# Centring moved back, last blocks in dead keys, setup signs on VectorE, and a wait in front of the gelu splits

## The reference

```
x = x + attn(layernorm(x))
x = x + ffn(layernorm(x))
attn: Q, K, V = x @ W.T + b      # W is 256 x 256
      scores = Q K^T / 16 * gaussian_mask(key position)
      out = softmax(scores) V, then @ Wo.T + bo
ffn:  h = gelu(x @ (alpha1 * sign(w1)).T + b1)      # 1024 wide
      out = h @ (alpha2 * sign(w2)).T + b2
```

## Time and profile before

| what | value |
|---|---|
| median of 3 runs | 1558.59 us |
| profiled execution | 1560.72 us, span 1558.9 us |
| mean granted TensorE clock | 0.97 |
| PE busy | 1465.9 us, 94% |
| DVE, POOL, ACT busy | 1098.1, 1045.1, 885.6 us (70, 67, 57%) |
| chain of waits | PE 70%, POOL 9%, DVE 7%, ACT 6%, DMA 3% |

### The profile page before, as it was taken

How to read it: one execution, slowest core, us unless ns; L and a number is a source line. 1 busy time by engine, 2 the same in 40 slices (tenths; PEclk the granted TensorE clock), 3 DMA queues, 4 the chain that set the end, 5 groups by cost and what they waited for, 6 DMA issues and landing times.

```text
span 1558.9 us, 21094 instructions
## 1 busy us (share of the span) xinstructions
PE 1465.9 (94%) x7709; PEld 1258.8 (81%) x7709; DVE 1098.1 (70%) x1574; ACT 885.6 (57%) x1238; POOL 1045.1 (67%) x1036
## 2 busy tenths in 40 slices
PE   7789999999898999989999899999999999899997
PEld 5678878788787878878788787878878788788886
DVE  6757766677776768867678776767766678666654
ACT  4566565565655656555565656666555565656433
POOL 4857757676676666766677676765766677576744
PEclk9899999999999999999999999999999999999998
DMA  6633707355062542606445063552716446072431
GB/s 194 97 81 55 154 9 118 99 79 138 22 130 66 95 122 49 152 17 109 109 80 137 10 122 85 89 129 36 144 37 109 108 65 152 1 122 68 70 66 28
DMA packets 107939, 138.50 MB, mean 89 GB/s; under 512 B 11822, under 2 KB 95164, under 8 KB 107836
## 3 DMA queue, kind: packets, MB, share of 16 engines
q1 hardware_dynamic: 107808, 137.15, 42.5%
q10 hardware_dynamic: 28, 0.01, 0.0%
HBM read 37.49 MB, written 16.78 MB: 35 GB/s over the span
## 4 chain that ended last, share of the span: by engine, by line
PE 70%; POOL 9%; DVE 7%; ACT 6%; DMA 3%; SPq 2%; issue 2%; DVEq 0%; POOLq 0%; ACTq 0%
PE ps L1009 19%; PE ps L983 17%; PE ps L1073 9%; PE ps L1086 6%; PE ps L1032 6%; PE ps L1087 5%; POOL kl L381 3%; DMA probs<-g 3%; POOL nmr L407 2%; SPq L306 2%; PE ps L1052 2%; ACT kh L500 2%; PE ps L963 2%; PE ps L964 2%; PE ps L966 2%
## 5 line engine op out<-in xcount | busy, mean ns | idle before, releaser
L389 POOL TENSOR_TENSOR probs<-probs 128x512 fp32r<-128x512 f32 x256 | 343.8, 1366 | 197.3 <-ACT probs L521 197.3
L1009 PE MATMUL ps<-probs,xnh 128*128 128x512 f32 x1024 | 286.0, 394 | 9.7 <-ACT probs L521 9.7
L1086 PE MATMUL ps<-sgn,probs 128*128 128x256 f32 x1024 | 250.9, 286 | 4.6 <-DVE ys L798 2.9
L1087 PE MATMUL ps<-sgn,probs 128*128 128x256 f32 x1024 | 249.1, 284 | 0.0
L754 DVE STREAM_TRANSPOSE probs<-probs 128x1024 f32<-128x1024 f32 x128 | 158.8, 1241 | 109.6 <-DMA probs<-g 108.2
L1009 PEld LDWEIGHTS ps<-probs,xnh 128*128 128x128 f32 x1024 | 190.2, 189 | 51.1 <-issue 13.3
L521 ACT ACTIVATE probs<-probs 128x1024 fp32r<-128x1024 f32 x128 | 135.7, 1060 | 153.1 <-DVE probs L754 152.5
L560 ACT ACTIVATE g<-ps,cols,alpha 128x512 f32<-128x512 f32 x256 | 183.5, 771 | 66.6 <-PE ps L1073 66.5
L515 ACT ACTIVATE g<-ps,nmax 128x1024 f32<-128x1024 f32 x128 | 142.1, 1112 | 123.6 <-DVE nmax L742 122.8
L742 DVE TENSOR_REDUCE nmax<-ps 128x1 f32<-128x1024 f32 x128 | 155.5, 1215 | 78.5 <-PE ps L983 78.2
L1086 PEld LDWEIGHTS ps<-sgn,probs 128*128 128x128 f32 x1024 | 197.0, 192 | 10.0 <-DVE ys L798 4.2
(11 more groups left out here) (115 smaller groups left out, 2770.3 us busy)
## 6 DMA issues: line engine op xcount, KB each, us to landing
probs<-g SPq DMA_DIRECT2D x512, 128.0 KB, 3.5
xrow<-in_L_attn_x_dram SPq DMA_DIRECT2D x32, 512.0 KB, 8.5
xin<-in_L_attn_x_dram SPq DMA_DIRECT2D x32, 512.0 KB, 8.7
out_dram<-xin SPq DMA_DIRECT2D x31, 512.0 KB, 4.5
regrouped_rows<-xn SPq DMA_DIRECT2D x120, 128.0 KB, 5.2
w1s<-in_L_ffn_w_dram SPq DMA_DIRECT2D x1, 1024.0 KB, 7.9
w2s<-in_L_ffn_w_dram SPq DMA_DIRECT2D x1, 1024.0 KB, 10.0
mask_bc<-mask_dram SPq DMA_DIRECT2D x1, 512.0 KB, 6.7
```

Source lines behind the costliest of these rows:

```text
L389: pool.tensor_tensor(ptl(b, q)[:, half(n)], pt(b, q)[:, half(n)], pth(b, q)[:, half(n)].bitcast(F32), ALU.subtract).then_inc(ptl_set, 1)
L1009: last = pe.matmul(ps[:, PV_BANK + c, :], xv[:, j, tile(c)], probs[:, lo, first:first + TH, tile(j)], start=k == 0, stop=k == len(parts) - 1)
L1086: pe.matmul(bank, probs[:, 0, r, tile(j)], sgn2[:, j, :], start=j == 0, stop=False)
L1087: last = pe.matmul(bank, probs[:, 1, r, tile(j)], sgn2[:, j, :], start=False, stop=j == J - 1)
```

## The change

- `center_attention(b+2)` on DVE moves from behind `lo_rows_ffn(b, 0)` to behind `row_max(b+1, 0)`.
- In front of `split_pair(b, 0)` DVE waits for `nmr2_set`, all eight of the batch (the roots of the second norm).
- Query tile 7 is regrouped into `last_regrouped`, which lies over `kl`; the wait for `pv_summed` moves from SP to DVE's `turn_probs(b, 7)`.
- PE does the scores of tiles 6 and 7 back to back, and `weigh_rows` steps 12 to 24 after them.
- Setup: the signs of w2 move from POOL to DVE, in two instructions; the means of |w2| move on ACT from the start to batch(0), in front of those of |w1|; `bvb` and `perm` are made earlier; the product for the bias and `Nh` goes ahead of `scores(0, 0)`; other instructions of the setup change places.

```diff
             def regrouped(b, q):
+                if q == T - 1 and b < B - 1:
+                    return last_regrouped[:, 0, :]
 # SP, regroup_probs
-                if q == T - 1 and b < B - 1:
-                    sp.wait_ge(pv_summed, N2 * b + 1)
-                elif q == T - 1:
+                if q == T - 1 and b == B - 1:
                     sp.wait_ge(kl_set, N2 * (b + 1))
                 if b == 0 and q == 5:
-                    sp.wait_ge(signs2_set, 1)
+                    sp.wait_ge(alphas_set, C)
 # POOL, setup
-            pool.tensor_scalar(sw2[:], w2s[:], 0.0, None, ALU.is_gt).then_inc(pos2_set, 1)
-            pool.wait_ge(alphas_set, C)
-            pool.tensor_scalar(w2s[:], w2s[:], 0.0, None, ALU.is_lt).then_inc(neg2_set, 1)
-            pool.tensor_tensor(sw2[:], sw2[:], w2s[:], ALU.subtract).then_inc(signs2_set, 1)
...
 # ACT, setup
             exponentials(0, 3)
+            normalize_attention(1, range(2, TH))
+            hi_probs(0, 1)
+            exponentials(0, 4)
             signs1(range(0, 2))
...
+            normalize_attention(1, tiles_of(1))
+            def mean_sizes():
+                act.wait_ge(signs_set, 2)
+                for c in range(C):
+                    act.activation(w2s[:, c, :], w2s[:, c, :], ACT.Abs, scale=1.0 / H,
+                                   accum_out=alpha2[:, c:c + 1]).then_inc(alphas_set, 1)
 # DVE, turn_probs
+                if q == T - 1 and b < B - 1:
+                    dve.wait_ge(pv_summed, N2 * b + 1)
 # DVE, setup
             turn_probs(0, 3)
+            dve.tensor_scalar(sw2[:], w2s[:], 0.0, None, ALU.is_lt).then_inc(neg_set, 1)
+            dve.wait_ge(neg_set, 2)
+            dve.scalar_tensor_tensor(out=sw2[:], in0=w2s[:], scalar=0.0, in1=sw2[:], op0=ALU.is_gt,
+                                     op1=ALU.subtract).then_inc(signs_set, 1)
 # DVE, batch
                 lo_rows_ffn(b, 0)
-                if b + 2 < B:
-                    center_attention(b + 2)
                 lo_outputs(b, 1)
                 invert_sums(b, 1)
                 for q in tiles_of(1):
                     add_attention(b, q)
+                dve.wait_ge(nmr2_set, T * (b + 1))
                 split_pair(b, 0)
...
                 row_max(b + 1, 0)
+                if b + 2 < B:
+                    center_attention(b + 2)
                 lo_rows_ffn(b, 1)
 # PE, batch, 0 < b < 15
-                    for i in range(TH):
-                        scores(b, TH + i)
-                        weigh_rows(b, 0, range(6 * i, 6 * i + 6))
+                    scores(b, 4)
+                    weigh_rows(b, 0, range(0, 6))
+                    scores(b, 5)
+                    weigh_rows(b, 0, range(6, 12))
+                    scores(b, 6)
+                    scores(b, 7)
+                    weigh_rows(b, 0, range(12, 24))
```

More of the change, by code:

```diff
@@ L73, in preln_attention_ffn @@
             sb("gap_kmf", [P, S], F32, place)
-            junk2 = sb("junk2", [P, C, H], F32, place)
+            sb("gap_j", [P, C, H], F32, place)
             sb("gap_b", [P, J // 2, D], F32, place)
@@ L85, in preln_attention_ffn @@
         kh = sb("kh", [P, N2, C, HALF], F32R)
+        with ExitStack() as place:
+            last_regrouped = sb("last_regrouped", [P, N2, S], F32, place)
         kl = sb("kl", [P, N2, C, HALF], F32R)
@@ L169, in preln_attention_ffn @@
             sem(n) for n in ("x2_turned", "x2h_set", "x2l_set", "hidden", "gelu_set", "gh_set", "gl_set"))
-        pos2_set, neg2_set, signs2_set = (sem(n) for n in ("pos2_set", "neg2_set", "signs2_set"))
         ffn_summed, ffn_scaled, y_set, table_loaded = (
@@ L596, in _ @@
             act.activation(Nh[:].rearrange("p c d -> p (c d)"), ps[:, 7, :], ACT.Copy).then_inc(nh_set, 1)
[L597 to L600, removed]
             exponentials(0, 1)
@@ L603, in _ @@
             exponentials(0, 2)
-            normalize_attention(1, range(2, TH))
             hi_probs(0, 0)
             exponentials(0, 3)
+            normalize_attention(1, range(2, TH))
+            hi_probs(0, 1)
+            exponentials(0, 4)
             signs1(range(0, 2))
[L608 to L611, removed]
+            exponentials(0, 5)
             hi_probs(0, 2)
+            hi_probs(0, 3)
             signs1(range(2, 2 * C))
[L614 to L618, removed]
+            normalize_attention(1, tiles_of(1))
[4 more added lines that the diff above has]
+                                   accum_out=alpha2[:, c:c + 1]).then_inc(alphas_set, 1)
                 for j in range(J):
@@ L639, in batch @@
                     exponentials(b, 5)
+                if b == 0:
+                    mean_sizes()
                 hi_probs(b, 4)
-                if b == 0:
-                    mean_sizes1()
                 exponentials(b, 6)
@@ L821, in _ @@
                                      op1=ALU.subtract).then_inc(ml_set, 1)
+            dve.wait_ge(consts_set, 5)
+            for c in range(C):
+                dve.tensor_scalar(bvb[:, c, :], ones[:], bv_c[:, c:c + 1], None, ALU.mult).then_inc(bvb_set, 1)
+            dve.tensor_copy(perm[:].rearrange("p (g r) -> p g r", r=QUAD),
+                            ident[:].rearrange("p (r g) -> p g r", r=QUAD)).then_inc(perm_set, 1)
             for n in range(N2):
@@ L834, in _ @@
             dve.tensor_scalar(sw1[:], w1s[:], 0.0, None, ALU.is_lt).then_inc(neg_set, 1)
+            row_max(0, 1)
+            center_attention(1)
             dve.wait_ge(neg_set, 1)
@@ L837, in _ @@
                                      op1=ALU.subtract).then_inc(signs_set, 1)
[L838 to L842, removed]
+            row_max(0, 2)
+            turn_probs(0, 0)
+            row_max(0, 3)
             dve.wait_ge(nh_set, 1)
@@ L845, in _ @@
                               Nh[:].rearrange("p c d -> p (c d)").bitcast(F32), ALU.subtract).then_inc(nl_set, 1)
-            row_max(0, 2)
-            turn_probs(0, 0)
-            row_max(0, 3)
             turn_probs(0, 1)
@@ L853, in _ @@
             dve.tensor_tensor(bias_bc[:], ps[:, 6, 0:D], bias_bc[:], ALU.add).then_inc(bias_set, 1)
+            row_max(0, 5)
             turn_probs(0, 2)
-            row_max(0, 5)
             turn_probs(0, 3)
[L857 to L861, removed]
+            dve.wait_ge(w2_loaded, 16)
+            dve.tensor_scalar(sw2[:], w2s[:], 0.0, None, ALU.is_lt).then_inc(neg_set, 1)
+            dve.wait_ge(neg_set, 2)
+            dve.scalar_tensor_tensor(out=sw2[:], in0=w2s[:], scalar=0.0, in1=sw2[:], op0=ALU.is_gt,
+                                     op1=ALU.subtract).then_inc(signs_set, 1)
             def batch(b, more):
@@ L882, in batch @@
                 if b == 0:
+                    dve.wait_ge(alphas_set, C)
+                    for c in range(C):
+                        dve.tensor_scalar(diag[:, c, :], ident[:], alpha2[:, c:c + 1], None, ALU.mult).then_inc(diag_set, 1)
                     dve.wait_ge(alpha2_spread, 1)
@@ L1121, in _ @@
             last.then_inc(wo_turned, 1)
-            scores(0, 0)
             pe.wait_ge(woT_set, 1)
@@ L1138, in turn_signs1 @@
                     last.then_inc(signs_turned, 1)
-            scores(0, 1)
-            scores(0, 2)
-            turn_signs1(range(0, 2))
             pe.wait_ge(bvb_set, C)
@@ L1146, in _ @@
             last.then_inc(bias_summed, 1)
-            scores(0, 3)
+            for q in range(TH):
+                scores(0, q)
+            turn_signs1(range(0, 2))
             scores(0, 4)
@@ L1161, in turn_signs2 @@
                     if k == 0:
-                        pe.wait_ge(signs2_set, 1)
+                        pe.wait_ge(signs_set, 2)
                     if k < 2:
@@ L1175, in batch @@
                     weigh_rows(b, 0, range(0, 6))
+                    scores(b, 6)
                     turn_signs2(range(0, 2))
-                    scores(b, 6)
                     weigh_rows(b, 0, range(6, 12))
```

5 lines of the change are left out of this document (removed).

## The result

The changed kernel takes **1550.06 us** (median of 5 runs, 1544.87 to 1552.51), the kernel before 1559.85 us on the same chip. The ratio is 0.9934 with an interval of 0.9907 to 0.9961: 0.7% faster. The forecast was 1548. The profiled execution has a span of 1548.3 us and a mean granted clock of 0.975.

The account below looks back on a forecast made before the run. PE bounds the kernel, so time is won only where it idles or runs at its lower clock. -12 + 2.9 + 1.5 - 3 = -10.7 gives 1550.0 profiled, 1548 us as median; range 1508 to 1569, likeliest case 1537 to 1559.

Parts of the forecast that it names:

- stall at `project` gone: PE's wait at project(b, 1) for DVE's lo_outputs, behind the centring: shrinks from 3.3 us to 0.3 in batches 0 to 13.
- next stall without the wait: PE's transposes L1052, late because of POOL's roots: idle 1.26 us, as the old batch 14 shows, unless DVE waits for them.
- new stall, hidden pair 4: PE waits for DVE's L781, late because the first split waits for roots and meets POOL's subtraction: 3.0 us, 15 times.
- clock: PE's lower granted clock after the new stall: 1.7 us a batch, in proportion to the old 1.9; bounds 0 and 3.3.
- a batch, times 14: Batches 0 to 13: 93.2 us each against 94.1, so -0.9 a batch and -12 us in all.
- batch 14: The batch with no centring to move, so nothing to win: 93.2 against 90.3 us, +2.9.
- end: Batch 15, bound by split 3 before ffn_row(0): splits start 1.8 us later, +1.5 us in all, bounds 0 and +3.
- setup: Start up to batch 1's queries: DMAs 5.7 us earlier, less 2.1 for means of |w2| and 0.6 for clock: -3.
- dead keys, score order: Last block regrouped into dead keys, and scores 6 and 7 back to back: both costed at nothing.
- rival A: Old stall goes, L781 late by only 1.0 us, no clock loss: 89.5 a batch, 1492 us; chance 0.17 with half-way cases.
- Rival B: Slower: POOL's third subtraction precedes split 2's TENSOR_TENSOR, stall 4.0, clock 2.2, 94.7 a batch, 1571 us; chance 0.11.

## Why the prediction was right

The mechanism was the one forecast, and the sum came out to 0.1 in the profiled executions (-10.7 and -10.7; the medians of five differ by 9.8). That closeness is luck: its terms were off by -2.2 (start), +1.2 (the fourteen intervals), +1.8 (batch 14) and -0.8 (end), which cancel, and the last two hang on where the clock happened to fall.

| step | predicted | measured | in short |
|---|---|---|---|
| stall at `project` gone | 3.3 to 0.3 | not in the list of waits | right |
| next stall without the wait | 1.26 at the transposes | 1.3 and 1.26 in the two kernels without it | right |
| new stall, hidden pair 4 | 3.0, 15 times | 3.06 in the steady batches, 2.98 in batch 14 | right |
| clock | 1.7 a batch | 1.6 | right |
| a batch, times 14 | 93.2, -12 | 93.33, -10.8 | right |
| batch 14 | +2.9 | +4.7 | undersized |
| end | +1.5 | +0.7; 2.1 like for like in clock | right in kind, a little undersized |
| setup | -3 | -5.2 (-6.5 from the queries of batch 0) | undersized |
| dead keys, score order | 0 | 0 within the error | right |

*The new stall.* The chain through batch 14's times put CAST and TENSOR_TENSOR at 3.97 us behind a wait; they took 3.99 (1418.38 to 1422.37). It put the split 1.8 later, and it waited 1.69. What decided between 1.0 and 3.0 was whether POOL's subtraction holds the split up. The kernel with the subtractions late settles it: same wait, stall 1.21 instead of 3.06. It also comes near rival A's time (1496.6, forecast 1492): the rival was wrong on what POOL does at that instant, not on what it would be worth. Rival B needed POOL's third subtraction ahead of split 2's TENSOR_TENSOR. That one starts at 1424.87 and the subtraction at 1425.42: the 0.4 us of the forecast were 0.55.

By the Trainium skill, page "SBUF — State Buffer", section "Who interferes with whom", whichever of DVE and GpSimd issues first holds the shared port pair for its whole instruction, and the other waits. The trace agrees: POOL starts 0.08 ahead, the CAST takes 1.1 more (1.76 for 0.66) and ends at 1420.14, the TENSOR_TENSOR takes 1.0 more, and both are back at 0.69 and 1.23 where no POOL instruction meets them.

*The clock.* Behind the 2.98 us stall PE runs at 0.50 (1.2 GHz) for 6.8 us, as it did behind the 3.3 us stall of before. Proportion gave 1.7 a batch and 1.6 came. That it isn't proportion over the whole way is shown by the kernels whose stall is 1.2 to 1.3 us: their steady stretches are at 1.00. And it is a mean: single stalls of 3.06 were followed by 1.00, 0.75 or 0.50 over 6.8 us.

*Batch 14.* It was given an average share of clock, 1.7. In the profiled run the low clock struck it in full: 6.8 us at half rate is up to 3.4. The three kernels with this stall in batch 14 show all three cases for the same part: 93.78 at clock 1.00, 95.34 at 0.98 and 96.76 at 0.96, where the kernel before takes 92.09. The first is +1.7, which is just the stall (3.01 for 1.26). So the term is +1.7, +3.2 or +4.7 as the clock falls, and +2.9 lies between. In a single batch a mean is a poor forecast.

*The end.* The measured +0.7 is two things. PE idles 2.1 more (64.26 - 51.90 = 12.36 against 63.58 - 53.34 = 10.24), near the 1.8 by which the splits were to start later, and its busy time is 1.4 shorter, for the kernel before runs at 0.50 for 3.4 us at the start of this part and the changed one doesn't. With the same low clock at this place the wait costs 2.1 (65.68 against 63.62): inside the bounds of 0 and +3, above the 1.5.

*The setup.* This is the term that was furthest off in size. The chain of waits after, at the start (start us, length us, what):

```profile
60.64 3.49 DMA regrouped_rows<-xn
...
66.50 2.09 ACT w2s L610 x4
...
70.52 3.48 DMA probs<-g
...
80.65 0.47 PE ps L962
```

The last DMA of batch 1's rows is over at 64.13; the one of before took 6.53 and ended at 71.38. That is 7.2 earlier where the chain of the prediction had 5.7. Of it 4.2 is the start: before, SP issues eight other DMAs (57.78 to 62.84) right ahead of these four; after, the eight are out by 54.57, and SP waits for ACT's rows until 58.74. The other 3.0 are the transfer itself, whose shortening the prediction left out. From there to PE's queries it is 16.5 us where it was 14.5. The two means of |w2|, 2.09, are on the path and ahead of tile 5's DMAs, as forecast. But the path is another one: it runs over these DMAs (3.48) and no longer over the means of |w1| (2.02), so that the difference of 2.0 is near the 2.1 of the forecast partly by chance, and the 0.6 for the clock can't be read from it. So -7.2 + 2.0 = -5.2, against -5.7 + 2.1 + 0.6 = -3. Why the transfer is shorter was not tried by itself.

## What to carry to other kernels

A wait that takes a fault away (here 2.55 us off POOL's root pair) has a price where it stands: ask not only how long it holds its engine, but which instruction of the neighbour it now releases at the same instant. 1.85 of the 3.06 us came from that meeting, and one wait on POOL, in a place with time to spare, took it away. And weigh a stall on PE with its clock: the edit that traded a 3.3 us stall for one of 3.06 at another place won 0.8 a batch, those that left 1.2 won 4.2. If work is ready (here split 0), try the wait behind it: that was worth another 0.5 a batch.

## What the hardware did that was not expected

- Stalls of 1.21 to 1.3 us a batch leave the steady stretch at 1.00, those of 3.06 take 1.6 us a batch more. Size alone doesn't say whether the clock falls: it stayed at 1.00 behind three of the changed kernel's fifteen stalls. With the wait alone, second stalls of 1.6 to 2.3 us follow the first by some 19 us, and the clock fell behind two of fourteen (1.83 and 1.89 us, at 0.53 from 1278.8 to 1282.3 behind one). In the last batch of before, waits of 1.11 and 0.52 us close together were followed by 0.50 for 3.4 us. What decides is open.
- Kernels with a stall of some 3 us spread by 4 to 11 us from run to run (the changed one 1544.87 to 1552.51), those without by 1 to 3.5. Batch 14 shows one reason: 93.78, 95.34 or 96.76, as the clock falls.
- Tiny POOL instructions pay the full price of meeting a split: two `nmr` instructions of one element per partition take 0.50 or 3.05 us together, the root of two elements 0.70 or 1.69.
